# Graph convolutions: shared sums of the edge runs added to their target columns by VectorE instead of by one-hot products

## What is computed

```python
deg  = segment_sum(ones, col, n);  dinv = rsqrt(deg)
norm = dinv[row] * dinv[col]                  # self loops are added to the edges
def conv(h, W, b): return segment_sum((h @ W.T)[row] * norm[:, None], col, n) + b
h   = relu(conv(x, W1, b1))
h   = relu(conv(h, W2, b2))
out = conv(h, W3, b3)
x   = x + out
```

## Time and profile before

| | us |
|---|---|
| median of 3 runs (lowest to highest) | 5152.69 (5146.39 to 5154.1) |
| the profiled execution, span from first to last instruction | 5143.9 |
| PE busy, share of the span | 3848.2 (75%) |
| DVE busy | 2174.4 (42%) |
| ACT busy | 1234.4 (24%) |
| POOL busy | 1935.0 (38%) |
| the convolutions, from PE's first product (2566.6) to the start of the next block's PE work (3491.0) | 924.4 |

### The profile page before, as it was taken

How to read it: one execution, slowest core, us unless ns; L and a number is a source line. 1 busy time by engine, 2 the same in 40 slices (tenths; PEclk the granted TensorE clock), 3 DMA queues, 4 the chain that set the end, 5 groups by cost and what they waited for, 6 DMA issues and landing times. The chain is left out here.

```text
span 5143.9 us, 62246 instructions
## 1 busy us (share of the span) xinstructions
PE 3848.2 (75%) x19117; PEld 2836.3 (55%) x19117; DVE 2174.4 (42%) x6089; ACT 1234.4 (24%) x3514; POOL 1935.0 (38%) x2021
## 2 busy tenths in 40 slices
PE   3877777234735555458399999996969999999597
PEld 2555555112425444357366665654538887777586
DVE  5555556600344444242300000005237777777723
ACT  3555454200100000012200000001125554444332
POOL 3455453474266666445400000001224444444053
PEclk8778888566866766668699999997579999999598
DMA  6655553000023333036454444443434444444266
GB/s 213 175 148 141 150 152 107 1 19 1 3 83 91 92 89 91 25 112 184 143 153 142 142 136 141 140 133 99 113 126 137 134 137 135 133 130 129 69 218 208
DMA packets 424073, 613.62 MB, mean 119 GB/s; under 512 B 149273, under 2 KB 287650, under 8 KB 423490
## 3 DMA queue, kind: packets, MB, share of 16 engines
q1 hardware_dynamic: 310578, 327.46, 22.2%
q0 software_dynamic: 104112, 273.76, 18.6%
q10 hardware_dynamic: 9056, 8.43, 0.5%
HBM read 517.83 MB, written 91.59 MB: 118 GB/s over the span
## 5 line engine op out<-in xcount | busy, mean ns | idle before, releaser
L2217 POOL DMA_INDIRECT stage<-t_row,f_take x168 | 162.1, 965 | 1269.7 <-POOLq L2064 1152.3
L865 POOL DMA_INDIRECT eg_rows<-t_edge,src_i x416 | 393.5, 946 | 563.7 <-DVE eg_pre L1698 422.1
L1108 PE MATMUL ps<-sum_hot,sum_rows 128*128 128x128 f32 x1664 | 330.0, 364 | 365.6 <-issue 201.5
L1372 PE MATMUL ps<-cv_cells,xn 128*128 128x384 f32 (+2 forms) x1600 | 535.7, 493 | 67.2 <-DMA cv_cells<-t_cells 67.2
L271 POOL DMA_INDIRECT t_cells<-times_seen,cell x416 | 409.8, 985 | 413.0 <-PEq L312 152.8
L865 POOL DMA_INDIRECT ag_rows<-t_att,src_i x416 | 401.7, 966 | 386.7 <-DVE ag_msg L970 264.6
L1108 PEld LDWEIGHTS ps<-sum_hot,sum_rows 128*128 128x128 f32 x1664 | 292.7, 264 | 403.0 <-issue 392.9
L865 POOL DMA_INDIRECT sum_rows<-t_row,src_i x416 | 393.9, 947 | 211.3 <-issue 116.5
L1050 PE MATMUL ps<-featT,ag_msg 128*128 128x128 f32 x1664 | 370.7, 357 | 127.2 <-issue 124.4
L1372 PEld LDWEIGHTS ps<-cv_cells,xn 128*128 128x128 f32 x1600 | 304.2, 190 | 279.5 <-DMA cv_cells<-t_cells 67.6
L1650 PE MATMUL ps<-eg_w,eg_rT 128*128 128x256 f32 x1664 | 439.3, 386 | 1.1 <-ACT eg_rT L1668 1.1
(11 more groups left out here) (418 smaller groups left out, 6296.4 us busy)
## 6 DMA issues: line engine op xcount, KB each, us to landing
cv_cells<-t_cells SPq DMA_DIRECT2D x225, 384.0 KB
cv_cells<-t_cells SPq DMA_DIRECT2D x75, 448.0 KB
xn<-in_L_ffn_W SPq DMA_DIRECT2D x57, 512.0 KB
t_cells<-zeros SPq DMA_DIRECT2D x17, 1664.0 KB
xn<-in_L_ffn_expert_w SPq DMA_DIRECT2D x110, 256.0 KB
ag_trow<-t_dst SPq DMA_DIRECT2D x104, 256.0 KB
t_cells<-zeros POOLq DMA_DIRECT2D x8, 1664.0 KB
eg_eaT<-in_edge_attr SPq DMA_DIRECT2D x208, 64.0 KB
```

The lines of the kernel that those rows point to most:

```text
L865: nc.gpsimd.indirect_dma_start(out=rows[:, j, :], out_offset=None, in_=table, in_offset=bass.IndirectOffsetOnAxis(ap=src_i[:, n:n + 1], ax ...
L1108: mm = nc.tensor.matmul(ps[:, j % BANKS, k * EC:(k + 1) * EC], lhs, hot[:, j, :], start=True, stop=True)
L1372: mm = nc.tensor.matmul(ps[:, bank(q, k, half), 0:at.stop - at.start], source(l)[:, s, k * 128:(k + 1) * 128], cells[:, n % CR, at], start ...
L2217: nc.gpsimd.indirect_dma_start(out=xd[:, j, :], out_offset=None, in_=t_row, in_offset=bass.IndirectOffsetOnAxis(ap=take_row[:, n:n + 1], a ...
```

## The change

Four things change, all within the convolutions:

- **Where the shared sums are formed.** `shared_products` and its five loads stand ahead of source tile 21 of quarter 0 (`SHARED_AT = NT - 4`), not behind tile 24. The transpose, the second ACT copy and all `close` matmuls are gone, and `own_head` with its iota and comparison.
- **Who adds them.** POOL clears `featT` (2 x 3200 columns) once for each layer, in layers 1 and 2 after the last `weigh` of the layer before. ACT copies the 128 shared columns to `shared`. DVE then adds them one after the other (`add_heads`): for each head an add of 128 x 2 elements at a column that comes from a register, each waiting for the one before it, with a load of four registers for every four heads.
- **Who evicts.** `keep` moves from ACT (copy) to DVE (add of PSUM to the cleared and head-filled `featT`), behind `add_heads` in DVE's program, and waits for the last product of the quarter.
- **One more DMA.** SP loads the 128 heads (4 bytes each, from 128 rows of the `dst` runs) ahead of the first cells.

```diff
             def load_number(l, q, s):
-                return LOADS * l + NT * q + (NT // SP_LOT if q > 0 else 0) + s
+                if q == 0:
+                    return LOADS * l + s + (NT // SP_LOT if s >= SHARED_AT else 0)
+                return LOADS * l + NT * q + NT // SP_LOT + s
...
                 @block.gpsimd
-                    nc.gpsimd.iota(own_head[:], [[1, N]], base=0, channel_multiplier=0, allow_small_or_imprecise_dtypes=True).then_inc(g.pool_step.sem, 1)
+                    for l in range(LAYERS):
+                        if l > 0:
+                            pool.wait_ge(g.y_ready.sem, g.y_ready.at(NT * l))
+                        nc.gpsimd.memset(featT[:, :, 0:N], 0.0).then_inc(g.table_clear.sem, 1)
 
                 @block.sync
+                    with nc.allow_non_contiguous_dma(reason="128 numbers"):
+                        sp.dma_start(heads[:].rearrange("a m r -> a (m r)"), io["dst_run"][:, 0:1].rearrange("p a -> a p")).then_inc(g.heads_in.sem, 16)
...
                 @block.tensor
-                                if q == 1 and s == 0 and bank(q, k, half) == 7:
-                                    pe.wait_ge(g.relu_done.sem, g.relu_done.at(2 * l + 2))
+                                if q == 1 and s == 0 and k == 0 and half == 0:
+                                    pe.wait_ge(g.shared_kept.sem, g.shared_kept.at(l + 1))
...
-                    def shared_turned(l):
-                        pe.wait_ge(g.relu_done.sem, g.relu_done.at(2 * l + 1))
-                        for k in range(KD):
-                            mm = nc.tensor.transpose(ps[:, 7, k * 128:(k + 1) * 128], shared[:, 0, k * 128:(k + 1) * 128], ident[:])
-                        mm.then_inc(g.core_ready.sem, 1)
-
-                    def close(l, q):
...
-                        for k in range(KD):
-                            for half in range(2):
-                                at = part(q, half)
-                                nc.tensor.matmul(ps[:, bank(q, k, half), 0:at.stop - at.start], shared[:, 1, k * 128:(k + 1) * 128],
-                                                 own_head[:, c0 + at.start:c0 + at.stop], start=False, stop=True).then_inc(g.agg_ready.sem, 1)
...
+                                if q == 0 and s == SHARED_AT:
+                                    shared_products(l)
                                 products(l, q, s)
-                                if q == 1 and s == 5:
-                                    close(l, 0)
...
-                            if q == 0:
-                                shared_products(l)
-                                shared_turned(l)
-                            else:
-                                close(l, q)
...
                 @block.scalar
+                    for l in range(LAYERS):
+                        act.wait_ge(g.used.sem, g.used.at(shared_load_number(l, NT // SP_LOT - 1) + 1))
+                        if l > 0:
+                            act.wait_ge(g.head_added.sem, g.head_added.at(128 * l))
+                        nc.scalar.copy(shared[:], ps[:, 4:6, 0:128]).then_inc(g.shared_kept.sem, 1)
+
+                @block.vector
+                    def add_heads(l):
+                        dve.wait_ge(g.table_clear.sem, g.table_clear.at(l + 1))
+                        dve.wait_ge(g.shared_kept.sem, g.shared_kept.at(l + 1))
+                        for m in range(128 // ER):
+                            for r, column in enumerate(head_columns(dve, nc.vector, m)):
+                                p = ER * m + r
+                                dve.wait_ge(g.head_added.sem, g.head_added.at(128 * l + p))
+                                at = featT[:, :, bass.ds(column, 1)]
+                                nc.vector.tensor_tensor(at, at, shared[:, :, p:p + 1], ALU.add).then_inc(g.head_added.sem, 1)
+                        dve.wait_ge(g.head_added.sem, g.head_added.at(128 * (l + 1)))
+
                     def keep(l, q):
                         c0 = QUARTERS[q][0] * P
+                        dve.wait_ge(g.used.sem, g.used.at(load_number(l, q, NT - 1) + 1))
                         for k in range(KD):
                             for half in range(2):
                                 at = part(q, half)
-                                act.wait_ge(g.agg_ready.sem, g.agg_ready.at(part_number(l, q, k, half) + 1))
-                                nc.scalar.copy(featT[:, k, c0 + at.start:c0 + at.stop], ps[:, bank(q, k, half), 0:at.stop - at.start]).then_inc(g.evicted.sem, 1)
+                                wide = featT[:, k, c0 + at.start:c0 + at.stop]
+                                nc.vector.tensor_tensor(wide, wide, ps[:, bank(q, k, half), 0:at.stop - at.start], ALU.add).then_inc(g.evicted.sem, 1)
+
+                    dve.wait_ge(g.heads_in.sem, g.heads_in.at(16))
                     for l in range(LAYERS):
+                        add_heads(l)
+                        for q, (t0, nt) in enumerate(QUARTERS):
                             keep(l, q)
```

53 lines of the change are left out of this document (24 added, 29 removed).

## The result

| | before | changed |
|---|---|---|
| median, us (5 executions each) | 5148.75 (5143.3 to 5154.1) | 5127.1 (5121.3 to 5128.64) |
| ratio, 95% interval | | 0.9951 (0.9938 to 0.9963) |
| profiled execution: span | 5143.9 | 5126.9 |
| its own time | 5145.62 | 5128.64 |

The account below looks back on a forecast made before the run. PE's end-to-end matmul stream was taken to bound the convolutions. Out of it: 23.2 + 5.5 + 1.2 + 2.7 = 32.6 us, less 0.5 for the heads' DMA, so 5152.7 - 32.1 = 5120.6 us; range 5113 to 5144.

Parts of the forecast that it names:

- 5116 to 5126: Whole kernel, in us: the forecast case of no or hardly any PE wait for the eviction; chance 0.60.
- the first rival: Quarter 0 of each layer: adds outlast their cover and PE waits; 5131, or 5146 at the bound; chance 0.27.
- The stream of PE: Convolutions: closings and the turning of the shared sums leave PE's matmul stream, 32.6 us in all, tail's 1.2 included.
- T: Start of a layer's shared products; the first weigh of quarter 0 was due at T + 60.2 us.
- The price of a closing: Convolutions: 8 close records cost PE 2.58 us by distance of starts, 2.76 in quarter 3.
- The chain against its cover: Ahead of each layer's first weigh: 128 DVE adds take 44.8 us against 45.6 of PE work; PE doesn't wait.
- The heads' DMA: Ahead of the first product: issuing this DMA before the first cells costs 0.5 us, between 0.3 and 1.3.
- The tail: End of layer 2's last quarter: DVE's four adds take 2.1 us, weigh starts 1.2 us earlier.
- The first stretch: Convolutions, from the first product to the start of layer 0's shared products; the prediction gave it no term.
- The step that failed: Start of the convolutions: removing the iota and comparison, which lay beside the first products, changes nothing.
- Behind the block stands a barrier and the later blocks are the same, so a gain is kept to the end: After the convolutions: their whole gain, 32.1 us, reaches the kernel's end.

## Why the prediction was right, and where it was not

The time, 5127.1, lies in the range of 5113 to 5144, but 1.1 us above the 5116 to 5126 that the forecast had at 0.60. It looks like the first rival, a chain a little late, and is not: no first `weigh` behind the adds waited. Some of the closeness is luck. The forecast of 5120.6 stands on a median of 5152.69 from three runs; on that of all five, 5148.75, the same 32.1 us give 5116.7, and the miss is 10.4 us instead of 6.5. As a gain, 21.7 were measured of 32.1. That PE's stream bounds the block, and that taking matmuls out of it pays one for one, was right. Of the terms:

- **The stream of PE.** From T to T, layers 1 and 2 start 306.74 us apart before and 295.33 after: 11.41 us for a layer, against 3 x 2.58 + 2.76 + 0.89 = 11.39 forecast. In layer 2 the same terms with the tail's 1.2 make 9.83, and up to the start of the last seven `weigh` it is 9.85. The price of a closing as the distance of starts was the right way to read the earlier trace rows.
- **The chain against its cover.** 45.0 us against 44.8 forecast, 0.30 and 0.51 apart as forecast, first add at T + 12.36 (12.2), `weigh` at T + 60.18 (60.2). The slack was a bit smaller than forecast: the eviction ends at T + 59.34, 0.84 ahead of `weigh` and 0.5 ahead of the load of its weights, for which the prediction had 0.8. The one add for each layer shows that the 128 cost PE nothing, and the shared sums three tiles later show what a missed cover costs. An add of two elements took 0.165 us, as large as the small ops of the earlier trace rows. By the table in the Trainium skill, "VectorE: DVE Perf Modes", section on the TRN2 errata, which the prediction weighed, it would be 62 ns, an estimate; the measurement decides.
- **The heads' DMA.** Forecast 0.5, measured 1.1 (1.0 when moved away). Its issue, 0.65, is like the earlier trace rows; that the first load also lands later by more than the slot was not in the sum. 0.6 us short.
- **The tail.** "together 2.1 us. So `weigh` starts at 3482.25, 1.2 us earlier": both right (2.06 us; 1.2 us). Failed: that it is then worth 1.2 us to the end. The longer pause lowered the clock for the matmuls behind it, 1.7 us.
- **The first stretch** cost 0.55 more. It varies by 1.6 us between the traces, so nothing follows.

Together 32.1 - 0.6 - 1.7 - 0.55 = 29.25, the block's measured gain (29.3).

- **The step that failed** is "The iota and comparison for the one-hot matrix lay beside the first products: nothing." The iota did lie there, and for that very reason it had been useful: it took the pair of MODIFY_POOL_CONFIG records and the 9 us behind them at a place where nobody waited, and the adds of a block more than a thousand us later had none. Taking it out left a pause of 7.4 to 8.3 us to the next add, which has gathers behind it in POOL's order. Price: 6.9 us in edge_gated (the mean of the seven with the change, 952.1, less 945.2 without), which is most of what is missing between the block's 29.3 and the medians' 21.7. The medians alone would not show it: their interval allows a gain of 19 to 32 us. The profile of before had a sign of it: the iota's row says 26.43 us of idle put down to issue, and the sequencer's pair stands 9 us ahead of it. I had read neither.
- "Behind the block stands a barrier and the later blocks are the same, so a gain is kept to the end" failed with it: barriers keep times apart, not the state in which an engine enters the next block.

What stays open: on the first chips the cause rests on ten traces, in which the block is long whenever the pair is in it, and the loss then arises right behind the pause, but there is no run there with the iota put back. Taking the iota away and putting it back moved the pair both ways, but on the chip with quicker gathers, where the pause costs only 1.4 us. Why the gathers are quicker there, and why the clock falls after some pauses of 2.25 us and not after others, was not looked into.

## What to carry to other kernels

Price a removed instruction not only by its own time: ask what it did first for its engine. Where an engine's instruction has a configuration record and a pause ahead of it, keep a tiny one of its kind early, in a place where nobody waits, and look where the pair of records stands after each change. Work moved from PE to another engine is free only up to the last add that fits under the stream: compare chain and cover to a microsecond, and count a pause of PE like those of 2.25 and 6.9 us here at more than its length, for the matmuls behind it may run at the lower clock (here 1.7 to 1.9 us more). Where a removed instruction moves such a pause to another engine's path, the block that pays can be a later one: compare all blocks, not only the one that was changed.

## What the runs showed of the hardware

- POOL's first iota or add after a PARTITION_ALL_REDUCE starts 7.1 to 9.5 us behind two MODIFY_POOL_CONFIG records, in all fourteen traces; memsets and indirect DMAs do not bring that on. The very first iota of the kernel starts 0.07 us behind such a pair.
- In edge_gated such a pause cost 6.9 us of the block on the first chips and 1.4 on the one with quicker gathers.
- PE's granted clock fell after a pause of 2.25 us in five executions and did not in two; after 6.9 us it fell all three times; after 0.68 and 1.2 us it stayed, three times each.
- DVE adds of two elements at a column from a register, each waiting for the last: 0.165 us long, 0.30 apart, 0.51 across a load of four registers.
- A matmul record of 16 columns costs 0.10 us in the stream (0.81 for eight), 0.32 at 384 columns.
- A DMA of 128 single numbers (4 bytes each) holds SP's queue for 0.70 us and delays the first product by 1.0.
